# Layer 1 softmax denominators: two pairs of heads in one bank, one reciprocal, division in parts of 32 rows

## What is computed

```python
q, k, v = heads of LN(x) @ Wq.T, LN(x) @ Wk.T, LN(x) @ Wv.T      # 16 heads, width 64
sim  = 50 * tanh((q @ k.T) / 8 / 50)                              # [head, 512, 512]
sim  = where(causal, sim, -inf);  attn = softmax(sim)
x    = x + LN((attn @ v) @ Wo.T)
r, k = sigmoid(xr @ Wr.T), relu(xk @ Wk.T) ** 2                   # xr, xk mix a token with the one before
x    = x + LN(r * (k @ Wv.T))
```

## Time and profile before

| | us |
|---|---|
| median of three runs | 1579.58 |
| lowest and highest | 1578.19, 1579.97 |
| the profiled execution | 1577.66 |
| its span, first to last instruction | 1575.7 |
| PE busy | 1484.3 (94%) |
| DVE busy | 1097.1 (70%) |
| ACT busy | 824.2 (52%) |
| POOL busy | 806.3 (51%) |

### The profile page before, as it was taken

How to read it: one execution, slowest core, us unless ns; L and a number is a source line. 1 busy time by engine, 2 the same in 40 slices (tenths; PEclk the granted TensorE clock), 3 DMA queues, 4 the chain that set the end, 5 groups by cost and what they waited for, 6 DMA issues and landing times.

```text
span 1575.7 us, 29502 instructions
## 1 busy us (share of the span) xinstructions
PE 1484.3 (94%) x10998; PEld 1069.2 (68%) x10998; DVE 1097.1 (70%) x1876; ACT 824.2 (52%) x1196; POOL 806.3 (51%) x1003
## 2 busy tenths in 40 slices
PE   3879999999999999999999999999999999999995
PEld 2546666666676767577767777777777777777774
DVE  5677787877777786855565748757586675774765
ACT  2344445354535444535556666656666565665641
POOL 4133535344444444334656657656576565755742
PEclk8788999999999999999999999999999999999998
DMA  7334343434343333110200010100101001000000
GB/s 164 61 42 68 42 82 42 82 41 80 40 80 40 67 41 66 70 68 1 74 14 1 1 41 1 41 1 1 40 0 40 0 0 40 0 15 13 1 27 13
DMA packets 46498, 60.82 MB, mean 39 GB/s; under 512 B 4912, under 2 KB 31952, under 8 KB 46416
## 3 DMA queue, kind: packets, MB, share of 16 engines
q1 hardware_dynamic: 45552, 59.03, 19.1%
q10 hardware_dynamic: 864, 0.66, 0.1%
HBM read 25.83 MB, written 8.39 MB: 22 GB/s over the span
## 4 chain that ended last, share of the span: by engine, by line
PE 86%; DVE 8%; ACT 3%; issue 2%; POOL 1%; DMA 0%; SPq 0%; POOLq 0%; DVEq 0%; ACTq 0%
PE psum L353 41%; PE psum L1745 9%; PE psum L1710 9%; PE psum L1761 6%; PE psum L999 5%; PE psum L1733 4%; PE psum L985 4%; PE psum L954 3%; DVE l_rowmax L823 2%; ACT l_probs L750 1%; PE psum L360 1%; PE psum L961 1%; PE psum L969 1%; PE psum L1019 1%; PE psum L1008 1%
## 5 line engine op out<-in xcount | busy, mean ns | idle before, releaser
L750 ACT ACTIVATE l_probs<-psum 128x512 f32<-128x512 f32 (+1 forms) x384 | 181.0, 524 | 207.7 <-PE psum L985 206.8
L1529 DVE RECIPROCAL l_att<-psum 128x512 f32<-128x512 f32 x64 | 214.6, 3354 | 55.1 <-PE psum L1733 50.8
L823 DVE TENSOR_REDUCE l_rowmax<-psum 128x2 f32<-128x1024 f32 (+3 forms) x256 | 200.5, 817 | 54.4 <-PE psum L961 54.0
L1445 ACT ACTIVATE l_probs<-psum 128x1024 f32<-128x1024 f32 (+1 forms) x192 | 163.7, 880 | 121.6 <-PE psum L1710 117.6
L227 POOL TENSOR_TENSOR l_pool_holder<-expo 128x1 f32<-128x1 f32 x128 | 26.0, 203 | 371.2 <-ACT l_probs L1451 199.0
L1520 DVE TENSOR_TENSOR l_qk_lo<-psum,l_qk_hi 128x1024 fp32r<-128x1024 f32 x64 | 77.9, 1217 | 176.2 <-ACT l_qk_hi L1435 176.2
L232 POOL TENSOR_SCALAR_AFFINE_SELECT l_probs<-l_probs 128x256 f32<-128x256 f32 (+1 forms) x384 | 176.4, 491 | 0.0
L1451 ACT ACTIVATE l_probs<-l_probs 128x2048 f32<-128x2048 f32 (+1 forms) x128 | 157.7, 1267 | 0.0
L1745 PE MATMUL psum<-l_probs,l_v 128*64 128x512 f32 (+3 forms) x1024 | 149.9, 435 | 0.0
L1745 PEld LDWEIGHTS psum<-l_probs,l_v 128*64 128x64 f32 x1024 | 71.4, 137 | 87.2 <-issue 75.3
L1377 POOL TENSOR_TENSOR l_keysum<-l_probs 128x768 f32<-128x768 f32 x62 | 113.9, 1836 | 6.2
(11 more groups left out here) (210 smaller groups left out, 4089.2 us busy)
## 6 DMA issues: line engine op xcount, KB each, us to landing
l_kT<-l_roped_hi SPq DMA_DIRECT2D x64, 128.0 KB, 4.2
l_qT<-l_roped_hi SPq DMA_DIRECT2D x64, 128.0 KB, 6.1
l_xin<-in_x SPq DMA_DIRECT2D x8, 512.0 KB, 4.1
l_kT<-l_roped_lo SPq DMA_DIRECT2D x32, 128.0 KB, 5.4
l_qT<-l_roped_lo SPq DMA_DIRECT2D x32, 128.0 KB, 6.6
l_x<-in_x SPq DMA_DIRECT2D x8, 512.0 KB, 4.0
x_mid<-l_x SPq DMA_DIRECT2D x8, 512.0 KB, 3.0
l_xin<-x_mid SPq DMA_DIRECT2D x8, 512.0 KB, 4.7
```

The costliest lines, as they stand in the source:

```text
L750: ring_s.free(nc.scalar.activation(probs[:, SLOT[p], e, c0:c1], ring_s.unit(*use)[:, 0:c1 - c0], ACT.Exp, scale=HD0 ** -0.5), *use)
L823: reduced = nc.vector.tensor_reduce(rowmax[:, t, a // 2, :, a % 2], ring_d.unit("max", a, k)[:, :, c0:c0 + (t + 1) * P], mybir.AxisListTyp ...
L1445: ring_s.free(nc.scalar.activation(probs[:, p % 2, :, c0:c1], ring_s.unit("score", p, u)[:, :, 0:c1 - c0], ACT.Tanh, scale=HD1 ** -0.5 / C ...
L1529: ring_d.free(nc.vector.reciprocal(att[p % 2][:], ring_d.unit("den", p)), "den", p)
```

## The change

1. `den` now works on two pairs at once (`den d` for the pairs 2d and 2d + 1). Four matrices of ones with 32 columns each send the denominators of the four heads to rows 0 to 31, 32 to 63, 64 to 95 and 96 to 127 of one bank, 512 columns each. There are 4 instead of 8 `den` pieces per batch.
2. One reciprocal per two pairs goes into a buffer of its own, `rden1`.
3. A head's 64 rows of numerators now find its reciprocals on 32 rows only, so `att` is four multiplications of 32 rows instead of one of 128.
4. `keysum` covers all 512 columns. POOL fills the first 128 by an extra instruction (`affine_select` from `probs`). ACT's tanh, which overwrites `probs`, now also waits for `sum` of the pair before it in that buffer.
5. The divided result `att` takes the same memory as the low part that is made from it. So `att p` waits until `o p - 2` has been computed.
6. All tables of order are new, for layer 0 too, and those of the seam.

```diff
-    keysum = sb("keysum", [P, 2, 2, T - P])
-    ones = sb("ones", [P, HD1])
+    keysum = sb("keysum", [P, 2, 2, T])
+    ones = sb("ones", [P, ROW0 // 2])
+    rden1 = sb("rden", [P, T])
...
-        "den": {(0,): 8.92, (1,): 11.98, (2,): 13.25, (3,): 17.31, (4,): 18.3, (5,): 24.22, (6,): 27.58, (7,): 28.88},
+        "den": {(0,): 11.02, (1,): 18.42, (2,): 22.09, (3,): 26.96},
...
         def keys(i, p):
-                ring_d.filled(pool, before, "den", q)
+                ring_d.filled(pool, before, "den", q // 2)
...
+            nc.gpsimd.affine_select(out=total[:, :, 0:P], in_=rows[:, :, 0:P], compare_op=ALU.is_ge, fill=0.0, base=0,
+                                    pattern=[[0, 2], [1, P]], channel_multiplier=-1)
...
         def score(i, p, u):          # ACT: tanh
                 ring_d.filled(act, before, "pv", q)
+                act.wait_ge(summed.sem, summed.at(before, 3 * q + 3))
...
-        def den(i, p):               # DVE
-            ring_d.free(nc.vector.reciprocal(att[p % 2][:], ring_d.unit("den", p)), "den", p)
+        def den(i, d):
+            ring_d.filled(dve, i, "den", d)
+            ring_d.free(nc.vector.reciprocal(rden1[:], ring_d.unit("den", d)), "den", d)
...
         def pv(i, p):                # DVE
-            ring_d.free(nc.vector.tensor_tensor(att[p % 2][:], att[p % 2][:], ring_d.unit("pv", p), ALU.mult), "pv", p)
+                    dve.wait_ge(att_used.sem, att_used.at(before, q + 1))
+            ring_d.freed(dve, i, "den", p // 2)
+            for e in range(2):
+                one = slice(ROW0 * (p % 2) + ROW0 // 2 * e, ROW0 * (p % 2) + ROW0 // 2 * (e + 1))
+                for row in (ROW0 * e, ROW0 * e + ROW0 // 2):
+                    rows = slice(row, row + ROW0 // 2)
+                    divided = nc.vector.tensor_tensor(att[p % 2][rows, :], ring_d.unit("pv", p)[rows, :], rden1[one, :], ALU.mult)
+            ring_d.free(divided, "pv", p)
...
-            pe.wait_ge(summed.sem, summed.at(i, 3 * p + 3))
-            for cols in (slice(0, P), slice(P, T)):
-                for e in range(2):
-                    weights = keysum[:, p % 2, e, :] if cols.start else probs[:, p % 2, e, cols]
-                    last = nc.tensor.matmul(ring_d.unit("den", p)[64 * e:64 * e + 64, cols], ones[:], weights,
-                                            start=True, stop=True, tile_position=(0, 64 * e))
+            pe.wait_ge(summed.sem, summed.at(i, 6 * d + 6))
+            for j in range(4):
+                rows = slice(ROW0 // 2 * j, ROW0 // 2 * (j + 1))
+                last = nc.tensor.matmul(ring_d.unit("den", d)[rows, :], ones[:], keysum[:, j // 2, j % 2, :],
+                                        start=True, stop=True, tile_position=(0, ROW0 // 2 * j))
```

More of the change, by code:

```diff
@@ L1109, in phase2 @@
     xT = [sb("xT" + s, [P, NC, T], F32R) for s in ("_hi", "_lo")]
-    att = [sb(f"att{k}", [P, T]) for k in range(2)]
     wq = split_weight("wq", [P, NC, F1], "left")
@@ L1115, in phase2 @@
     v1 = sb("v1", [P, NT, H1, HD1])
-    keysum = sb("keysum", [P, 2, 2, T - P])
-    attT = [sb("attT" + s, [P, 2, T], F32R) for s in ("_hi", "_lo")]
-    ones = sb("ones", [P, HD1])
+    keysum = sb("keysum", [P, 2, 2, T])
+    attT_high = sb("attT_hi", [P, 2, T], F32R)
+    with nc.sbuf_tensor("l1_att", [P, 2, T], F32) as divided:
+        pass
+    attT = [attT_high, sb("attT_lo", [P, 2, T], F32R)]
+    att = [divided[:, k, :] for k in range(2)]
+    ones = sb("ones", [P, ROW0 // 2])
+    rden1 = sb("rden", [P, T])
     norm_x = Norm(nc, sb, sig, expo, "x", 1)
@@ L1203, in phase2 @@
+        "key_out": {(): 43.07},
+        "square": {(): 44.64},
+        "kact_hi": {(): 43.58},
+        "kact_lo": {(): 44.75},
+        "out": {(): 47.08},
+        "gate_b": {(): 51.76},
+        "gate": {(): 46.6},
+        "x4_stats_b": {(): 53.62},
+        "x4_stats": {(): 48.84},
+        "x4_rstd_b": {(): 66.71},
+        "x4_rstd": {(): 51.03},
+        "x4_norm_b": {(): 65.03},
+        "x4_norm": {(): 54.17},
+        "store_b": {(): 57.19},
+        "store": {(): 49.6},
     }
@@ L1208, in phase2 @@
     prologue_table = {
[L1209 to L1214 removed]
+        "small": {(): 291.373},
@@ L1273, in phase2 @@
     s_uses = schedule.uses("v", "qk", "score", "x3_T", "r", "key", "out")
-    ring_d = Units(banks[0:2], schedule, {use: use for use in d_uses}, sem, "d")
+    ring_d = Units(banks[0:2], schedule, {use: use for use in d_uses}, sem, "d",
+                   {use: "inverted" if use[0] == "den" else "read" for use in d_uses})
     ring_s = Units([psum[:, 2:4, :], psum[:, 4:6, :]], schedule, {use: use for use in s_uses}, sem, "s",
@@ L1367, in keys @@
             rows = probs[:, p % 2, :, :]
-            tile0, tile1, tile2, tile3 = (rows[:, :, OFF1[kt]:OFF1[kt] + T - max(kt, 1) * P] for kt in range(NT))
-            tile0 = rows[:, :, P:T]
             total = keysum[:, p % 2, :, :]
@@ new lines, in den @@
+                    for j in range(4):
+                        last = nc.tensor.matmul(ring_d.unit("den", d)[ROW0 // 2 * j:ROW0 // 2 * (j + 1), kt * P:T], ones[:],
+                                                probs[:, j // 2, j % 2, OFF1[kt]:OFF1[kt] + T - kt * P], start=(kt == 0),
+                                                stop=(kt == NT - 1), tile_position=(0, ROW0 // 2 * j))
+                ring_d.fill(last, "den", d)
+                return
+            pe.wait_ge(summed.sem, summed.at(i, 6 * d + 6))
@@ L1737, in pv @@
+            ring_d.claim(pe, i, "den", d)
+            for j in range(4):
+                rows = slice(ROW0 // 2 * j, ROW0 // 2 * (j + 1))
+                last = nc.tensor.matmul(ring_d.unit("den", d)[rows, :], ones[:], keysum[:, j // 2, j % 2, :],
+                                        start=True, stop=True, tile_position=(0, ROW0 // 2 * j))
+            ring_d.fill(last, "den", d)
         def pv(i, p):
```

353 lines of the change are left out of this document (167 added, 186 removed).

## The result

The changed kernel takes 1598.55 us (median, 1591.77 to 1607.25), the kernel before 1578.88 us measured beside it. The ratio is 1.0126 with the interval [1.0105, 1.0147]: slower by about 20 us, where I had forecast 20 us faster. The profiled executions are 1600.94 (span 1599.2) and 1577.66 (span 1575.7).

A forecast was written before the change was run, and what follows sets the result against it. PE was taken to bound layer 1's passes. Denominators -29.4, pass waits +4.2, the end +4.6 and layer 0 at 0 gave -20.6 us: 1557 against the profiled execution, 1559 forecast as median, range 1547 to 1573.

The forecast's parts named there:

- The denominators on PE: Dens on PE: 62 at 0.914 us become 31 at 0.88, saving 29.4 us; changes of tiling cost nothing more.
- The passes: Layer 1's steady passes: about 98.0 us instead of 101.2, with 0.6 us of added PE waits in each.
- (a): Tanh starting late behind pv, three places a pass instead of one: 0.27 us each, 0.54 us a pass added.
- (b): Den waiting for both pairs' keysums in a pass: hidden, with slack of about 0.2 us.
- (c): Den, reciprocal, division, then the ring_d bank again: 6.3 us, hidden behind about 6.6 us of PE work.
- DVE beside POOL: DVE's load in a layer 1 pass: loses 13.4 us, gains 16.3, reaching 71 of about 98 us, not a bound.
- the rival of the held banks: Divisions in 32-row parts hold the banks, some 2 us a pass: +14 instead of +4.2, time 1569; chance 0.14.
- the choice between 2.72 and 2.46 us: Four 32-row divisions on DVE: 2.72 us without overlap, 2.46 with; 2.72 taken, said to move only the slack.
- The end: Last batch: last score to o 7 in about 21 us instead of 14.8; in all +4.6 us, bounds +2 and +8.
- Layer 0: Layer 0's new order of the same pieces: no reason for a sign, 0 us, bounds -5 and +5.

The follow-up runs named there:

- a_div128: a_heat with one division of 128 rows per pair in place of four of 32 rows, output not the layer's: 1571.16 us.
- a_scores: The changed kernel with the first units of scores 2, 5 and 7 in layer 1 moved behind the pv their tanh waits for: 1602.72 us.
- a_heat: The changed kernel with only filler products 1 and 2 of layer 0 moved back to where they stood before: 1582.77 us, ratio 1.0029.
- a_own_b: a_heat with the last batch's pairs 6 and 7 given their own denominators, reciprocals and 128-row divisions, normalization left in place: 1577.88 us, ratio 0.9996.

## Why the prediction was wrong, step by step

**The denominators on PE: right in kind, a little too cheap.** The four tiles overlap as the earlier trace rows said. In a pass, from the start of a den to the start of what follows, 8 old ones take 7.61 us and 4 new ones 3.98: 3.63 gained where I had 3.79. I had taken 0.88 for the changed den and it is 0.996; the 0.10 that I had seen as the price of another kind of product behind it belonged to it too.

**The passes: mis-sized.** 98.0 forecast, 99.73 measured. The waits by start-to-start times are 3 x 0.36 for tanh, 0.29 for a score behind x3_T' and 0.2 in smaller ones, 1.56 in all where the kernel before had 0.21: +1.35, where I had +0.6. The places (a) were right, their price was 0.36 instead of 0.27, and x3_T' with a score behind it I had not seen. Den's 0.16 comes on top. The remaining 0.8 us is spread over the points where one kind of product follows another; I counted the changes of tiling as 40 on both sides and so as nothing, and did not find out by a run what they cost.

**(b) and (c) in the steady passes: right.** No wait for keysums and none for a divided bank, a_div128 leaves the pass as it is, and a_scores shows how small the slack was.

**DVE beside POOL: a term that was missing, without a price in the loop.** I had DVE near 71 us a pass; it is 77.3. Reciprocals (13.4) and divisions (22.0) are as counted. But in the new order several small instructions stand beside POOL's additions and last until those end, here 1.38 us for one that took 0.17 before (timeline of the changed kernel):

```profile
1134.38 1.38 DVE L334 TENSOR_SCALAR l_x_veps<-l_x_mv 128x4 f32<-128x4 f32 x1
1133.90 1.83 POOL L1380 TENSOR_TENSOR l_keysum<-l_probs 128x768 f32<-128x768 f32 x1
```

Four instructions of L334 in a pass do so, and each ends within 0.05 us of a POOL addition.

**The first batch of layer 1: the step that was missing.** I took every pass for a steady one. The first has no work of a batch before it, so (c) was open at two places for 2.9 and 2.5 us, and in the changed kernel the clock fell behind both. It is the rival of the held banks, at a place where I had not looked. I had also written that the choice between 2.72 and 2.46 us for four divisions doesn't move the sum. It does: the end's sum has 2.72 twice, and 2.46 would take 0.5 us off it.

**The end: mis-sized, by a wait I left out.** Forecast 21 us from the last score to o 7, measured 23.2. Mask 7 done after 4.9 (5.0 forecast), den 2.3 (2.2), reciprocal 3.45 (3.45), four divisions 2.8 (2.7): all as worked out. The normalization took 3.6 us instead of 2.55, its first part standing beside POOL's subtraction. And pv 7 needs the bank that the division of pair 6 frees. I had its predecessors in the chain and not pv 7 itself, and its 2.3 us became 4.4 by the clock. The link between the two divisions was pv 7, not the normalization; at full clock it would have been the normalization with its 3.6 us, about 1 us earlier. All this is 2.3 of the 7.3 us by which the last stretch missed. Another 0.6 lie behind o 7 (0.9 us shorter than before, where I had 1.5). The other 4.4 lie ahead of the last score: I had 2.8 us less there for the denominators, and it is 1.6 us more. I didn't take that part apart.

**Layer 0: the step that failed.** "I see no reason for a sign and take 0, bounds -5 and +5" rested on one row, the longest kind of wait in the old order. Measured were +16.0 us. Two things were wrong in it. The waits of the new order were not worked out at all: PE is idle for 41.4 us from the third batch on instead of 28.2, 13 us more and far outside the bounds. And an order was priced by waits alone, though its clock could be read by stretch: even before, three stretches of layer 0 ran at 1.2 GHz, and the new table took the fillers away from where PE waits. Their place is worth 14 of the 16 us (a_heat), but not because the new order lost more to the clock than the old one had; it failed to win back what the old one was losing, and so its added waits were paid in full. What is left of a_heat's loss is 2 us: it reaches the third batch 2.1 us later than the kernel before (loading is ordered anew too), its next five passes are 2.4 us shorter, and from there to layer 1 it takes 2.3 us longer. I didn't take these apart.

Without layer 0 the sum would still have been wrong: a_heat is 4.4 us slower than the kernel before, not 20 us faster. By the profiled executions it is 26 us away from the forecast: 8.7 in the five passes, 8.0 in the first two batches, 7.3 in the last stretch, 2.0 before layer 1.

## What to carry to other kernels

Price a new order by its waits, worked out for that order and not read off the old one, and by the clock: find what keeps PE busy where it waits (fillers too), and see whether it still stands there. Follow a chain that is hidden in the loop once more through the first and the last pass, where the work that hides it is missing; joining two pairs saved PE 7.3 us in five passes, and the last stretch took 9.0 back. And an instruction that is moved for the end's sake by a table is moved in each pass.

## What the runs showed of the hardware that I had not expected

- A division of 32 rows and 512 columns takes 0.67 to 0.70 us, as long as one of 128 rows (0.68); four in a row do not overlap (2.79 us).
- A DVE instruction on 4 columns took 0.63 to 1.38 us instead of 0.17 where POOL was adding beside it, and ended with that addition.
- With single waits of 0.4 to 1.1 us, 3.15 us in all within 5.3 us and no filler among them, PE was granted 1.2 GHz until 404.6 us. With two pairs of filler products between the waits (a_heat) it stayed at 2.4 GHz. Behind the same two waits of 2.9 and 2.5 us in layer 1 the clock was at half for 13.6 us in the changed kernel, 3.4 in a_heat and not at all in a_own_b.
- A block of numerators took 4.49 us at 1.2 GHz and 2.36 at 2.4 GHz, pv 7 took 4.4 and 2.3. PE was busy 533.0 and 521.5 us with the same instructions of layer 0. Two numbers of a table were worth 15.8 us, more than the 7.3 us that the five steady passes gained.
